# Layer 0 of a four-layer kernel: the 3x3 convolution by four products for two columns, the heads' norm in two parts, half the query diagonal on ScalarE

## What is computed

```python
h = _layernorm(seq, ln_w, ln_b)
x_in, z = jnp.split(h @ w_up + b_up, 2, axis=-1)        # 384 each
x_act = silu(causal 4-tap filter of x_in)
q, k, v = x_act @ w_q, x_act @ w_k, x_in
hs = _mlstm_scan(q, k, v, gates)                         # 12 heads of 32, over 1024 steps
mu, var = hs.mean(-1, keepdims=True), hs.var(-1, keepdims=True)      # of each head
hn = (hs - mu) / jnp.sqrt(var + 1e-05) * mh_w + mh_b
h_out = (hn + skip * x_act) * silu(z)
y = seq + h_out @ w_down + b_down + silu(linear layer of the input)
out = batchnorm(3x3 convolution of y, 192 -> 192 channels, padded by one)
```

## Time and profile before

| | us |
|---|---|
| median of 3 runs | 8910.59 |
| lowest and highest | 8900.13, 8935.14 |
| the profiled execution | 8910.43 |
| its span, first to last instruction | 8908.6 |

### The profile page before, as it was taken

How to read it: one execution, slowest core, us unless ns; L and a number is a source line. 1 busy time by engine, 2 the same in 40 slices (tenths; PEclk the granted TensorE clock), 3 DMA queues, 4 the chain that set the end, 5 groups by cost and what they waited for, 6 DMA issues and landing times.

```text
span 8908.6 us, 92950 instructions
## 1 busy us (share of the span) xinstructions
PE 7634.6 (86%) x34478; PEld 3414.0 (38%) x34478; DVE 5789.4 (65%) x10165; ACT 3558.1 (40%) x6596; POOL 1941.1 (22%) x1640
## 2 busy tenths in 40 slices
...
PEclk9999999999999997669888888888989888888988
...
GB/s 64 35 37 36 36 36 41 36 40 46 44 41 39 37 34 71 4 72 122 151 128 116 158 144 97 165 150 107 159 157 124 119 152 139 107 164 140 103 222 142
DMA packets 244195, 849.57 MB, mean 95 GB/s; under 512 B 46412, under 2 KB 49176, under 8 KB 243360
## 3 DMA queue, kind: packets, MB, share of 16 engines
...
## 4 chain that ended last, share of the span: by engine, by line
PE 61%; DVE 22%; ACT 8%; DMA 3%; issue 3%; SPq 1%; POOL 1%; ACTq 0%; DVEq 0%; POOLq 0%
PE ps L2106 10%; PE ps L2566 5%; DVE arena L1818 4%; PE ps L2351 4%; PE ps L1053 4%; PE ps L1299 3%; PE ps L1023 3%; PE ps L2116 3%; PE ps L935 3%; PE ps L2577 2%; PE ps L2547 2%; PE ps L2237 2%; PE ps L1301 2%; DMA arena<-img,arena 2%; PE ps L1313 2%
## 5 line engine op out<-in xcount | busy, mean ns | idle before, releaser
L2384 POOL DMA_INDIRECT arena<-img,arena x1152 | 1378.3, 1196 | 2717.5 <-DMA img<-arena 1840.8
L2281 DVE SCALAR_TENSOR_TENSOR arena<-arena 128x384 f32<-128x384 f32 x1152 | 745.0, 647 | 653.1 <-DMA arena<-img,arena 649.7
L1818 DVE TENSOR_REDUCE arena<-ps 128x2 f32<-128x1024 f32 x768 | 894.8, 1218 | 327.4 <-PE ps L2085 324.7
L967 POOL TENSOR_TENSOR arena<-arena 128x512 f32<-128x512 f32 x384 | 439.0, 1148 | 2774.8 <-DMA arena<-decay 2774.8
L1959 ACT ACTIVATE arena<-ps 128x512 f32<-128x512 f32 x1536 | 818.0, 603 | 346.8 <-PE ps L2116 344.4
L2566 PE MATMUL ps<-arena 128*64 128x512 f32 x3072 | 834.9, 671 | 128.3 <-DMA arena<-arena 72.6
L2106 PE MATMUL ps<-arena 128*64 128x512 f32 x3072 | 938.1, 713 | 0.0
L2351 PE MATMUL ps<-arena 128*96 128x128 f32 x4608 | 617.8, 291 | 53.2 <-DVE arena L2270 53.0
L2351 PEld LDWEIGHTS ps<-arena 128*96 128x96 f32 x4608 | 564.5, 175 | 232.3 <-issue 231.9
L1053 PE MATMUL ps<-arena 128*128 128x512 f32 x768 | 442.0, 659 | 87.1 <-DVE arena L1073 47.2
L935 PE MATMUL ps<-arena 128*128 128x512 f32 x1152 | 507.2, 596 | 0.0
...
## 6 DMA issues: line engine op xcount, KB each, us to landing
arena<-arena SPq DMA_DIRECT2D x1024, 144.5 KB, 2.9
arena<-decay SPq DMA_DIRECT2D x384, 256.0 KB, 3.2
...
```

Of the source, the lines that this page charges most:

```text
L1818: dve.tensor_reduce(out, self.wides[B.at("max", b, g, n, h) // 2].rearrange("p (a b) -> p a b", a=2), AX.X, AL.max).then_inc(*S.mark("max_ ...
L2281: dve.scalar_tensor_tensor(gb[:, 0:384], gb[:, 384:768], pp[:, 1, n:n + 1], gb[:, 0:384], AL.mult, AL.add).then_inc(*S.mark("corner_x", b, n))
L2384: pool.indirect_dma_start(self.g[n % 6], None, img, bass.IndirectOffsetOnAxis(ap=ii[:, n:n + 1], axis=0)).then_inc(*S.landed(f"{self.tag}g ...
```

## The change

- The convolution is done by four products for two neighbouring columns: POOL forms four combinations of the padded image's columns (`pool_join`; `va` for 128 channels, `vb` for the last 64), DVE forms the matching filter sums once at the start (`u2`), and PE multiplies each for three filter rows, 256 columns at a time. Their outputs lie in two banks. ACT brings one of them out with the bias (`p1`), DVE adds and subtracts to get the even and odd columns and takes the statistics.
- The convolution comes in three groups of six steps: image half 0, half 1, and the last 64 channels. Each group holds two banks. Four steps stand ahead of `project`, two within, twelve in the recurrence.
- The heads' norm is done for chunks 0 to 3 within the recurrence, steps 16 to 23, and for chunks 4 to 7 behind it. `ahead` begins in step 4.
- The transposes and the gating of the first half (`pe_laid`, `dve_gated`) move from join into norm.
- The `zs` half of `enter` moves behind join, ahead of the convolution.
- In the recurrence ACT makes two of the four diagonal copies, and the scaling of the skip (before on DVE, L1103).

The core of the diff:

```diff
-        self.ypb = ar([128, 18, 34])
+        self.ya, self.yb = yr([128, 34, 34]), yr([128, 50, 34])
+        self.va = [z.rearrange("p a b -> p (a b)")[:, 0:2176].rearrange("p (q r n) -> p q r n", q=4, r=34) for z in self.zs]
...
+        self.vb = ar([128, 2, 34, 16])
+        self.u2 = ar([128, 2, 3, 192])
+        self.p1 = ar([128, 256])
...
+        for k in range(2):
+            u = self.u2[:, k]
+            g = [W["C2"][:, k, :].rearrange("p (y x n) -> p y x n", y=3, x=3)[:, :, x, :] for x in range(3)]
+            dve.tensor_tensor(u, g[0], g[2], AL.add).then_inc(*S.mark("prep0", "u", k, 0))
...
+            dve.tensor_tensor(u, u, g[1], AL.subtract).then_inc(*S.mark("prep0", "u", k, 1))
...
+            dve.scalar_tensor_tensor(g[1], u, 0.5, g[1], AL.mult, AL.add).then_inc(*S.mark("prep0", "u", k, 2))
...
+            dve.tensor_scalar(u, u, 0.5, None, AL.mult).then_inc(*S.mark("prep0", "u", k, 3))
...
             dve.wait_ge(*S("s_pe", b, n - 3))
-            for j in range(4):
+            for j in range(2):
                 i = dve.tensor_copy(qd[32 * j:32 * j + 32, j, :], qq[32 * j:32 * j + 32, g, sl])
             i.then_inc(*S.mark("qd", b, n))
...
+        def diagonal(n):
...
+            act.wait_ge(*S("s_pe", b, n - 3) if n > 2 else S("s_pe", b - 1, 21 + n))
...
+            for j in range(2, 4):
+                i = act.activation(qd[32 * j:32 * j + 32, j, :], self.qq[32 * j:32 * j + 32, g, sl], ACT.Copy)
+            i.then_inc(*S.mark("qd_act", b, n))
...
+        diagonal(0)
...
                 act.wait_ge(*S("zero", "later", b, n))
+                if n < 23:
+                    diagonal(n + 1)
...
+                if g == 1 and c in (1, 2, 3):
+                    act.activation(self.xa[:, c - 1, :], self.xa[:, c - 1, :], ACT.Identity, scale=self.W["SK"][:, c - 1:c], bias=self.W["MB"][:, c - 1:c]).then_inc(*S.mark("o_act", b, c, "skip"))
...
+        num, den, sq = self.norm_parts(part)
...
+        if part:
+            self.filter = self.dve_filter(dve, b + 1) if b + 1 < self.NB else iter(())
+            dve.wait_ge(*S("pv_pe", b, 23))
+        dve.wait_ge(*S("o_act", b, 4 * part + 3))
+        dve.tensor_reduce(s_, num, AX.X, AL.add).then_inc(*S.mark("norm_dve", *key, "sum"))
...
+        if part:
+            self.dve_gated(dve, b, 0, 0)
+        yield
+        if part:
+            self.dve_gated(dve, b, 0, 1)
...
+        dve.tensor_tensor(v_, v_, s_, AL.mult).then_inc(*S.mark("norm_dve", *key, "var"))
+        if part:
+            self.dve_gated(dve, b, 0, 2)
...
+        dve.tensor_tensor(sq, num, bc(v_, 32), AL.mult).then_inc(*S.mark("norm_dve", *key, "out"))
+        if part:
+            run(some(self.filter, 3))
...
+    def pe_norm(self, pe, b, part):
+        if part:
+            self.pe_laid(pe, b, 0)
+        yield from skip(8)
+    def pe_laid(self, pe, b, h):
+        S, B = self.S, self.B
+        o = self.sq1.rearrange("p a b -> p (a b)")
+        pe.wait_ge(*S("norm_dve", b, h, "out"))
+        for g in range(3):
+            ps, free = B.take(("hn", b, h, g), ("join_dve", b, "skip", 3 * h + g))
+            pe.wait_ge(*free)
+            for c in range(4):
+                i = pe.transpose(ps[:, 128 * c:128 * c + 128], o[:, 384 * c + 128 * g:384 * c + 128 * g + 128], self.C["ID"])
+            i.then_inc(*S.mark("laid_pe", b, h, g))
+    def dve_gated(self, dve, b, h, g):
+        S, qt, zs = self.S, self.qt, self.zs[b % 2]
+        n = 3 * h + g
+        dve.wait_ge(*S("laid_pe", b, h, g))
+        dve.wait_ge(*S("o_act", b, 3, "skip"))
+        dve.scalar_tensor_tensor(qt[:, g, H(h)], self.B("hn", b, h, g)[:, :], self.W["MW"][:, g:g + 1], self.xa[:, g, H(h)], AL.mult, AL.add).then_inc(*S.mark("join_dve", b, "skip", n))
+        dve.wait_ge(*S("join_dve", b, "skip", n))
+        dve.tensor_tensor(qt[:, g, H(h)], qt[:, g, H(h)], zs[:, g, H(h)], AL.mult).then_inc(*S.mark("join_dve", b, "gate", n))
...
+        self.pe_laid(pe, b, 1)
...
+        for g in range(3):
+            self.dve_gated(dve, b, 1, g)
+        for n, inner in enumerate((self.ya[:, 1:17, 1:33], self.yb[:, 17:33, 1:33], self.ya[:, 17:33, 1:33])):
...
+        act.activation(yb[0:64, 33:49, 1:33], yb[64:128, 17:33, 1:33], ACT.Copy).then_inc(*S.mark("halo", b, 0))
+        act.activation(yb[64:128, 1:17, 1:33], yb[0:64, 17:33, 1:33], ACT.Copy).then_inc(*S.mark("halo", b, 1))
...
+    def pool_join(self, pool, b):
+        S, ya, yb, va, vb = self.S, self.ya, self.yb, self.va[b % 2], self.vb
+        parts = ((0, 2, AL.subtract), (1, 2, AL.add), (2, 1, AL.subtract), (3, 1, AL.subtract))
+        pool.wait_ge(*S("laid_pe", b, 1, 2))
+        pool.memset(ya, 0.0)
+        pool.memset(yb, 0.0).then_inc(*S.mark("zero", "pad", b))
+        for key, r0, r1 in (("upper", 0, 17), ("last", 0, 34), ("lower", 17, 34)):
+            if key == "last":
+                pool.wait_ge(*S("conv_pe", b - 1, 2))
+                pool.wait_ge(*S("halo", b, 1))
+                for n, q in enumerate((0, 3, 1, 2)):
+                    h, (i, j, op) = n // 2, parts[q]
+                    if n == 2:
+                        pool.wait_ge(*S("parts", b, "upper"))
+                    r, y = slice(64 * h, 64 * h + 64), yb[64 * h:64 * h + 64, 16 - 16 * h:50 - 16 * h, :]
+                    t = pool.tensor_tensor(vb[r, n % 2], y[:, :, i:i + 31:2], y[:, :, j:j + 31:2], op)
+            else:
+                pool.wait_ge(*S("join_dve", b, "y", 0 if key == "upper" else 2))
+                if key == "lower":
+                    pool.wait_ge(*S("parts", b, "last"))
+                for q, (i, j, op) in enumerate(parts):
+                    t = pool.tensor_tensor(va[:, q, r0:r1, :], ya[:, r0:r1, i:i + 31:2], ya[:, r0:r1, j:j + 31:2], op)
+            t.then_inc(*S.mark("parts", b, key))
...
+        for n in range(3):
+            banks = []
+            for q, by in enumerate(("first", "y")):
+                ps, free = B.hold(("conv", b, n, q), ("conv_dve", b, n, by))
+                pe.wait_ge(*free)
+                banks.append(ps)
+            out = [banks[q in (1, 2)][:, 256 * (q in (2, 3)):256 * (q in (2, 3)) + 256] for q in range(4)]
+            m = slice(128, 192) if n == 2 else slice(0, 128)
+            halves = list(enumerate(both)) if n == 2 else [(n, slice(0, 128))]
+            for y in range(3):
+                for n2, pair in enumerate(((0, 1), (3, 2))):
+                    rows = lambda h: slice(16 * h + y, 16 * h + y + 16)
+                    for q in pair:
+                        for h, r in halves:
+                            pe.matmul(out[q][r, :], part(0, y, q, m), flat(va[:, q, rows(h), :]), start=y == 0 and n2 == 0, stop=False)
+                    for t, q in zip(both, pair):
+                        for h, r in halves:
+                            i = pe.matmul(out[q][r, :], part(1, y, q, m)[t], flat(vb[t, n2, rows(h), :]), start=False, stop=y == 2 and n2 == 1)
+                    if y == 2 and n2:
+                        i.then_inc(*S.mark("conv_pe", b, n))
+                    yield
+            for q in range(2):
+                B.drop(("conv", b, n, q))
...
+            act.activation(self.p1, self.B("conv", b, n, 1)[:, 0:256], ACT.Identity, bias=self.W["C2B"][:, n // 2:n // 2 + 1]).then_inc(*S.mark("conv_act", b, n))
...
+            dve.tensor_tensor(y, one.rearrange("p (s n) -> p s n", s=2), self.p1.unsqueeze(1).to_broadcast([128, 2, 256]), AL.add).then_inc(*S.mark("conv_dve", b, n, "first"))
...
+            dve.tensor_tensor(y[:, 0, :], y[:, 0, :], two[:, 256:512], AL.add)
+            dve.tensor_tensor(y[:, 1, :], y[:, 1, :], two[:, 256:512], AL.subtract).then_inc(*S.mark("conv_dve", b, n, "y"))
+            dve.wait_ge(*S("conv_dve", b, n, "y"))
             dve.bn_stats(self.stats[:, n, b, :], self.yo[:, n, :]).then_inc(*S.mark("conv_dve", b, n))
...
-            g = ahead(b + 1) if b + 1 < NB else iter(())
+            g, early = ahead(b + 1) if b + 1 < NB else iter(()), norm(b, 0)
             for n, _ in enumerate(chunks(b)):
                 yield
-                if n > 7:
+                if n > 3:
                     next(g, None)
-            run(g)
+                if n > 15:
+                    next(early)
...
-        run(enter(0))
+        run(enter(0, 0))
         for b in range(NB):
             g = conv(b - 1) if b else iter(())
-            run(some(g, 5))
+            run(enter(b, 1))
+            run(some(g, 4))
             p = project(b)
             run(some(p, 8))
             run(some(g, 2))
             run(p)
-            weave((scan(b), 24), (g, 11))
+            weave((scan(b), 24), (g, 12))
             if b + 1 < NB:
-                weave((norm(b), 8), (enter(b + 1), 6))
+                weave((norm(b, 1), 8), (enter(b + 1, 0), 3))
             else:
-                run(norm(b))
+                run(norm(b, 1))
             join(b)
         run(conv(NB - 1))
     def pe(self, e, NB):
...
```

(2 more changed lines are left out.)

240 lines of the change are left out of this document (95 added, 145 removed).

## The result

The changed kernel takes 8854.5 us (median of 17 runs) against 8914.3 of the kernel before (17 runs): ratio 0.9938, 95% interval 0.9927 to 0.9948. That is 0.6% less, where the prediction has 2.1% and a range that ends at 8805. The profiled execution took 8835.2 us, its span is 8833.4.

A forecast was written before the change was run, and what follows sets the result against it. The prediction took PE's own work to set the time nearly everywhere, with its waits that count in layer 0 being for DVE. Its terms: 8910.4 - 240 + 15 x 3 + 6 - 1 = 8720 us, 2.1% less; range 8640 to 8805.

The forecast's parts named there:

- Part 1: Convolution on PE: 44.9 us a block falls to 29.9, saving 15.0 us a block, 240 us over 16.
- The rival's smaller form: Last 64 channels' convolution: products on the four quarters don't overlap, +41 us, 8761; no chance of its own given.
- Part 2: Norm and join: three PE waits, 4.1 us in all against 4.2 before, so a net change of zero.
- Part 3: POOL's column combinations ahead of the convolution: hidden behind PE's work with about 3.5 us to spare.
- Part 4: Recurrence: new waits of PE less those gone, net +4.2 us listed, +1.3 by an event order; +3 us a block taken.
- the late wait: PE's wait of 3.1 to 3.7 us for DVE late in the recurrence, forecast to go; with a small one, -3.6 us.
- The half-rate stretches I leave as they are: Recurrence: PE's stretches at 1.2 GHz, costing 5.3 us a block before, taken as unchanged.
- The prediction's own test: Signs in the changed trace that would make it wrong: a block over 198 us, or half-rate stretches over 10 us a block.
- Part 5: Kernel's ends: filter sums at the start +6 us, last block -1 us, digit string 0.
- Another limit holds the block at 205 us: Rival for the whole block: the gain is not there at all, 8905 us; chance 0.03.
- DVE and ACT set the pace: Rival in the recurrence: scores wait for two engines, net 8 to 9 us a block, 8795 to 8810 us; chance 0.25.
- The waits go with the work: Rival in the recurrence: waits hidden by convolution steps, the 1.2 GHz stretch goes, 8620 to 8660 us; chance 0.17.

The follow-up runs named there:

- b_fill: The kernel before plus 12 idle products of 116 columns (2.7 us) in the wait ahead of the score of step 21; ratio 0.9948.
- a_fill4: The changed kernel plus idle products of constants (12, 5, 5, 4) in four of PE's waits; ratio to the kernel before 0.9875.
- a_best: a_three3 plus idle products of constants in the waits left, 7.7 us a block; ratio to the kernel before 0.9742.
- a_three3: The changed kernel, last convolution group a step later, last 64 channels' combinations on DVE, first half's third gating earlier; ratio to the kernel before 0.9817.
- a_diag3: The changed kernel with the whole query diagonal on DVE again, ACT's half taken out; ratio to the kernel before 0.9938.
- b_half_fill: The kernel before with half of its convolution left out and 12 idle products ahead of the score of step 21; ratio 0.968.
- b_half: The kernel before with its convolution's products on 256 columns in place of 512; 8737 us, ratio 0.9792.

## Why the prediction was wrong, step by step

The sum puts a block at 193 us (205.4 less 15.0, and 3 of waits). It takes 205.8: 5.3 us more of waits and 7.3 of half rate than the sum has.

**Part 1, the convolution: right.** PE's timeline of the first group, which begins at half rate and reaches the full one by the third step, against the earlier trace rows:

```profile
1512.80 1.92 PE L1386 MATMUL ps<-arena 128*128 128x256 f32 x4 [2.60 <-POOL arena L1354]
1514.65 1.23 PE L1389 MATMUL ps<-arena 64*128 64x256 f32 x4
1515.81 1.41 PE L1386 MATMUL ps<-arena 128*128 128x256 f32 x4
1517.15 0.70 PE L1389 MATMUL ps<-arena 64*128 64x256 f32 x4
1517.78 1.13 PE L1386 MATMUL ps<-arena 128*128 128x256 f32 x4
1518.84 0.70 PE L1389 MATMUL ps<-arena 64*128 64x256 f32 x4
1519.47 0.70 PE L1386 MATMUL ps<-arena 128*128 128x256 f32 x2
```

1519.47 - 1517.78 = 1.69 us, as forecast. The first step, 3.01 us, is the same at half rate: a conv step behind the wait costs 1.3 us more. And the last 64 channels, against the earlier trace rows:

```profile
1429.67 1.08 PE L1386 MATMUL ps<-arena 128*64 128x256 f32 x8
1430.69 0.66 PE L1389 MATMUL ps<-arena 64*64 64x256 f32 x8
1431.28 1.13 PE L705 MATMUL ps<-arena 128*128 128x512 f32 x2
```

1.61 us (forecast 1.59): products on the four quarters do overlap, eight records in 0.59 us. The rival's smaller form falls.

**Part 2, join: the sum right, by errors that cancel.** The prediction has three waits of 1.4, 1.3 and 1.4 us, 4.1 in all. Measured are 1.2, 2.5 and 0.3, 4.0 in all (means over the fourteen blocks): the bank of the heads, the lin banks, and the last gating, which PE waits for in three blocks only.

```profile
PE ps L1252 <- DVE arena L1411: 16.5, 14, 1.2
PE ps L1296 <- DVE arena L1263: 4.2, 3, 1.4
```

```profile
1482.27 3.65 PE L1278 MATMUL ps<-arena 128*128 128x512 f32 x4 [2.48 <-DVE arena L1261]
```

That the sum fits is luck. The lin banks' wait is longer because the third gating stands in DVE's queue behind the reduction of the squares, which waits for ACT's squaring. It also has a price that the sum left out: the four records then take 3.6 us in place of some 1.9, half rate again.

**Part 3, POOL: the step that failed by its cover.** POOL and DVE after the first sum of join:

```profile
1496.77 4.92 POOL L1354 TENSOR_TENSOR arena<-arena 128x272 f32<-128x272 f32 x4 [3.73 <-DVE arena L1315]
1501.65 7.69 POOL L1348 TENSOR_TENSOR arena<-arena 64x544 f32<-64x544 f32 x4
1509.49 3.25 POOL L1354 TENSOR_TENSOR arena<-arena 128x272 f32<-128x272 f32 x4
```

```profile
1498.93 0.68 DVE L1315 TENSOR_TENSOR arena<-ps,arena 128x512 f32<-128x512 f32 x1
1499.53 3.24 DVE L757 SCALAR_TENSOR_TENSOR arena<-arena 128x1024 f32<-128x1024 f32 x2
...
1504.34 6.09 DVE L757 SCALAR_TENSOR_TENSOR arena<-arena 128x1024 f32<-128x1024 f32 x3
```

The eight last instructions take 10.9 us where the prediction has 7.0, just past the "half as long again" that it called still hidden. That alone would expose 0.4 us, not 2.6. POOL also begins them 2.0 us after the second sum ends (1499.6), not 1.3, since its first four, at 1.2 us each and not 0.6, are still running; and PE gets there 10.6 us after that sum, not 12. The prices alone were right. The profile's line over all of L1348 (duration in ns, lowest, median, highest):

```profile
L1348 POOL TENSOR_TENSOR arena<-arena x64: 1085/2013/2099, 268.9 to 3331.9; 64x544 f32<-64x544 f32 x64
```

1.09 us is the price without company (forecast 1.15): four of the 64, the ones that DVE's work doesn't cover whole, take 1.09 to 1.11. The sixty beside DVE's filter take 2.07 in the median. For L1354 it is 0.63 and 1.61.

**Part 4, the recurrence: the waits came, their price didn't.** The bank wait of the last group is 3.25 us (forecast 3.2), the late wait is gone, the wait for the first score fell from 1.92 to 1.42:

```profile
1409.47 1.08 PE L1386 MATMUL ps<-arena 128*64 128x256 f32 x8 [3.25 <-DVE arena L1414]
...
1418.08 3.75 PE L696 MATMUL ps<-arena 128*128 128x512 f32 x4 [2.60 <-DVE arena L495]
```

The wait for the mean is 2.60 here and 2.8 in the mean of the blocks, with 2.2 forecast (1.06 before and 1.1 more); the norm in steps 16 to 23 costs some 2.1 us, not 3.5, of which 1.3 stand ahead of the score of step 18; a wait of 1.37 us for the first bank of group 1 (for DVE's L1119) wasn't foreseen.

In all the idle time rose by 8.3 us and not by 3. The recurrence's share is 6.0, where the list in the prediction adds up to 4.2 and 3 was taken, as a middle between it and another estimate. Over the list are group 1's bank (1.4), the small waits of 0.2 to 0.7 us between steps 5 and 15 (1.8 in place of 0.5) and the mean (1.7 in place of 1.1); under it is the norm (2.1 in place of 3.5). The other 2.3 are join and POOL, forecast at zero. 5.3 us are 80 us in fifteen blocks.

The larger part failed in one sentence of Part 4: "The half-rate stretches I leave as they are". The term is put at nothing. The cost of the stretches before was known, 5.3 us a block, and so was what they stand behind the earlier trace rows; the sum had new waits of 3.2 and 2.2 us, took away the late one, and added no stretch. The runs show 26.6 us a block at half rate in place of 11.9. L696 above shows the price: its four records take 3.7 us, where 1.9 is usual for four of 512 columns. That is 7.3 us a block, 110 in all (6.2 and 93 with idle time counted once). The fills show that the waits bring it: b_fill, a_fill4 and a_best leave the order of the other work as it is, put idle products into waits, and half-rate time falls from 11.9 to 5.6, from 26.6 to 16.3 and, from a_three3, from 15.1 to 2.2. The prediction's own test names both: "A block over 198 us, or half-rate stretches of more than 10 us a block". The second sign is too weak to tell anything: the kernel before has 11.9 already.

**Part 5, the ends: right in layer 0** (5.7 us later for 6), wrong on the digit string, which the prediction puts at 0 and the runs at 28 us in its block and at 2 to 27 us in the whole kernel. Without it the miss would be larger.

**The rivals.** "Another limit holds the block at 205 us" names the measured length of a block, and is wrong: the equal length is a sum that happened to come to zero, and blocks of 187.6 to 208.9 us were made. "DVE and ACT set the pace" has the nearest time, 8795 to 8810. It had longer waits and one more stretch at half rate, both of which came, but it had one stretch where there are several, and the diagonal's wait for two engines that it rests on is worth nothing (a_diag3). "The waits go with the work" was the wrong way round.

**What stays open.** What follows the second block of the later layers, 26 us shorter in the two traces, wasn't settled: in two sets of runs the traces with the new string are 12 to 55 us shorter there than one with the old, in a third (a_best against b_half_fill) 11 us longer. Norm in one part wasn't tried alone, so the gain of that step isn't known. Nor is it known what makes a stretch at half rate 3.4 us long at one wait and 6.8 at another: the longest of the four waits (3.25 us) has 3.4, the mean's (2.6 to 3.1) mostly 6.8.

## What to carry to other kernels

When work is taken off a PE that is nearly full, price each wait that is left or new at its length and at what the following products cost at half rate, in most blocks 1.7 to 3.4 us here for a wait of 2.5 to 3.3 us, and more where less work stood around it (b_half). Waits of 1.0 to 1.4 us in a row count too. List the new waits first, with the slower engine's prices taken beside its neighbour, not alone. Where a wait can't be removed, products of constants that fit into it cost nothing and kept the clock up; count them in records, since a fill that overruns the wait gives all of it back.

## What the runs showed of the chip

- Adding work made both kernels faster: 2.7 us a block in the wait of the kernel before, 0.9948; 9.6 in the changed one, 0.9875 in place of 0.9938.
- The time at half rate behind the late wait of a block (3.2 us before, 3.7 then) grew from 7.6 to 13.4 us in the mean, and to 20.5 in six of fourteen blocks, when half of the convolution was left out; filling that wait then gave 7.4 us a block.
- POOL's own instructions slow down beside DVE as DVE's do: 1.1 to 2.07 us for 64x544, while DVE's multiply-adds of 1024 columns went from 1.28 to 2.01. The Trainium skill (GPSIMD Engine Reference, Key points) says that GpSimd shares its SBUF interfaces with VectorE. The trace agrees, and shows the cost on both sides; the prediction had used it for DVE's side only.
- Moving four of POOL's instructions to DVE cost DVE 3.97 us and took 7.7 from POOL, where they ran beside DVE's filter; without that company one takes 1.1 us on POOL.
